# Attention scores as three products of 64 rows instead of two of 128, in pairs over the halves of the array, with turns and scores taken two by two

## The reference, cut to what matters

```python
q = x @ Wq + bq;  k = x @ Wk + bk;  v = x @ Wv + bv      # 8 heads of 64 columns
scores  = einsum('bdsh,bdth->bdst', q, k) / sqrt(8)       # 2048 x 2048 per head
weights = softmax(scores, axis=-1)
feats   = einsum('bdst,bdth->bdsh', weights, v)
x = layernorm(x + feats @ Wo + bo)
# then a mixture of experts: sigmoid gate, the best 6 of 64 experts, 256 places each,
# h = silu(g) * v of width 64, a shared expert of width 128, and a second layernorm
x = layernorm(x + shared + routed)
```

## Time and profile before

| what | value |
|---|---|
| runs, median (lowest to highest) | 1288.0 us (1287.32 to 1289.65) |
| the profiled execution, its own time | 1288.48 us |
| its span in the profile | 1286.7 us |
| busy share of the span | PE 97%, PEld 72%, DVE 69%, ACT 56%, POOL 30% |
| share of the chain that ended last | PE 88%, DVE 5%, DMA 3%, issue 2% |
| that chain by line | L1674 18%, L1642 17%, L1655 16%, L1476 11% and more |
| granted clock of TensorE | 0.996 of 2.4 GHz |

### The profile page before, as it was taken

One profiled execution on the slowest core, in us unless ns is written; L12 is line 12 of the kernel. 1 busy time (PEld: TensorE's weight loads), 2 busy tenths in 40 slices (PEclk: granted clock), 3 DMA queues, 4 the chain that ended last, 5 costly groups with the idle time before them and its releaser, 6 DMA issues.

```text
span 1286.7 us, 23210 instructions
## 1 busy us (share of the span) xinstructions
PE 1243.3 (97%) x8004; PEld 927.9 (72%) x8004; DVE 889.9 (69%) x1693; ACT 721.3 (56%) x1243; POOL 381.4 (30%) x434
## 2 busy tenths in 40 slices
PE   7999999999999999999999999999998999999896
PEld 5888777767777777767777777777766777777642
DVE  5622566667777868777767868767775777777387
ACT  5520366656555646646555655656623777787434
POOL 0000001212422322231331331331343666666412
PEclk9999999999999999999999999999998999999999
DMA  8788454534534543553543453563688999997598
GB/s 272 258 295 276 137 135 143 148 110 131 138 96 101 140 130 81 143 123 87 153 124 93 131 145 71 154 169 112 175 305 324 387 386 386 350 333 263 225 427 347
DMA packets 105059, 257.42 MB, mean 200 GB/s; under 512 B 26904, under 2 KB 53464, under 8 KB 101616
## 3 DMA queue, kind: packets, MB, share of 16 engines
q1 hardware_dynamic: 84720, 201.12, 50.3%
q0 software_dynamic: 17920, 50.62, 10.5%
q10 hardware_dynamic: 2304, 4.20, 0.8%
HBM read 182.26 MB, written 134.98 MB: 247 GB/s over the span
## 4 chain that ended last, share of the span: by engine, by line
PE 88%; DVE 5%; DMA 3%; issue 2%; POOL 1%; ACT 0%; SPq 0%; DVEq 0%; POOLq 0%; ACTq 0%
PE pv_acc L1674 18%; PE slot L1642 17%; PE slot L1655 16%; PE slot L1476 11%; PE slot L1740 5%; PE slot L1692 5%; PE misc L1538 4%; PE pv_acc L1476 3%; PE misc L1476 3%; PE slot L1782 2%; DMA got<-y_hbm 2%; DVE prob L1347 1%; DVE picked L1220 1%; PE misc L1583 1%; DVE base L1437 1%
## 5 line engine op out<-in xcount | busy, mean ns | idle before, releaser
L1004 ACT ACTIVATE prob<-prob,row_min 128x1024 f32<-128x1024 f32 x256 | 293.3, 1146 | 69.1 <-DVE prob L1347 62.5
L990 ACT ACTIVATE p_t<-slot 128x512 f32<-128x512 f32 x256 | 151.7, 592 | 293.1 <-PE slot L1642 291.4
L1655 PE MATMUL slot<-k_stack,q_stack 128*128 128x512 f32 x1024 | 299.9, 415 | 0.0
L1330 DVE COPY p_t<-slot 128x512 f32<-128x512 f32 x256 | 175.1, 684 | 165.7 <-PE slot L1642 164.5
L1642 PE MATMUL slot<-ident,prob 128*128 128x128 f32 x2048 | 269.3, 275 | 2.0 <-ACT prob L1004 2.0
L1642 PEld LDWEIGHTS slot<-ident,prob 128*128 128x128 f32 x2048 | 231.4, 141 | 52.4 <-issue 28.8
L1674 PE MATMUL pv_acc<-p_t,v_all 128*64 128x256 f32 x2048 | 235.2, 382 | 0.0
L1674 PEld LDWEIGHTS pv_acc<-p_t,v_all 128*64 128x64 f32 x2048 | 141.5, 137 | 90.8 <-issue 26.3
L844 POOL TENSOR_TENSOR moved<-acc,moved 64x256 f32<-64x256 f32 x63 | 46.0, 730 | 530.5 <-DMA moved<-acc 530.4
L1655 PEld LDWEIGHTS slot<-k_stack,q_stack 128*128 128x128 f32 x1024 | 173.7, 190 | 24.1 <-DVE p_t L1330 1.1
L1347 DVE TENSOR_SCALAR_CACHE_REDUCE prob<-slot,row_min 128x1024 f32<-128x1024 f32 x128 | 163.8, 1280 | 12.7 <-PE slot L1655 12.7
(11 more groups left out here) (196 smaller groups left out, 1698.8 us busy)
## 6 DMA issues: line engine op xcount, KB each, us to landing
disp_hbm<-zero_hbm SPq DMA_DIRECT2D x64, 518.0 KB, 6.2
rows_all<-disp_hbm SPq DMA_DIRECT2D x64, 518.0 KB, 9.6
y_hbm<-zero_hbm SPq DMA_DIRECT2D x48, 512.0 KB
got<-y_hbm SPq DMA_DIRECT2D x15, 1536.0 KB, 19.3
q_stack<-q_hbm SPq DMA_DIRECT2D x128, 128.0 KB, 4.5
up_pair<-in_L_ffn_w_up SPq DMA_DIRECT2D x26, 512.0 KB, 7.8
down_w<-in_L_ffn_w_down SPq DMA_DIRECT2D x32, 256.0 KB, 9.7
q_hbm<-q_hi SPq DMA_DIRECT2D x8, 512.0 KB, 2.8
```

The lines of the kernel that those rows point to most:

```text
L990: e.activation(p_t[m % 2][u][:, 0:2, :], view[:, 0:2, :], ACT.Copy).then_inc(a_pt, 1)
L1004: e.activation(keys, keys, ACT.Exp, bias=row_min[:, me % 2, j, 1:2], scale=-1.0, accum_out=row_sum[:, me % 2, j, half:half + 1]).then_inc( ...
L1330: e.tensor_copy(p_t[m % 2][u][:, 2:4, :], view[:, 2:4, :]).then_inc(v_pt, 1)
L1655: made = e.matmul(slot[:, n * BANK:(n + 1) * BANK], qs[:, part, j * P:(j + 1) * P], k_stack[:, ms % H, keys], start=part == 0, stop=part == 1)
```

## The change: what it does

- **Scores.** Each step has three products over 64 rows in place of two over 128: hi·hi, hi·lo and lo·hi (lo·lo is gone). The two banks of a step use different row halves of the array, and the matmuls alternate between them: 6 matmuls of 64 rows x 512 columns, each with its own weights.
- **Keys.** `k_rows` takes the place of `k_stack` with the same number of bytes. Keys for one bank lie in partitions 0 to 63 and for the other in 64 to 127. To get the shifted rows, the second half of each projection uses weights that are moved on by 64 columns; Wk is passed in with its first 64 columns repeated at its end (576 columns), and the bias with a rolled copy. ScalarE and VectorE write `k_rows` as 128 partitions x 512.
- **Order.** PE, DVE and ACT take two turns and then two scores, in even rounds only; the ring follows. Side jobs come between turns and scores, and after the scores. The two v pieces that are left for the attention come after the first two scores.
- **Around it.** Loads of the last chunk come up to 4 rounds later, since heads are done with their memory later; the load of pair 9 of the experts' weights also waits for the last projection, as that of pair 10 did.

```diff
@@ buffers
-        k_stack = sb("k_stack", [P, H, T], F32R, att)
+        k_rows = sb("k_rows", [P, H, 2, 2, BANK], F32R, att)
-        w_raw[0] = sb("w_raw0", [P, KC, C], F32, raw_k)
+        w_raw[0] = sb("w_raw0", [P, KC, C + D], F32, raw_k)
@@ order of the slots
-        for s in range(LAST + LAG):
-            takes += ([("turn", s - LAG)] if s >= LAG else []) + ([("scores", s)] if s < LAST else [])
-            takes += [("v", NS - V_LATE + s)] if s < V_LATE else []
+        for s in range(0, LAST + LAG, 2):
+            takes += [("turn", s - LAG), ("turn", s - LAG + 1)] if s >= LAG else []
+            takes += [("scores", s), ("scores", s + 1)] if s < LAST else []
+            takes += [("v", NS - V_LATE + s), ("v", NS - V_LATE + s + 1)] if s < V_LATE else []
@@ where keys lie
+        def keys_of(h, half, bank):
+            p, odd = divmod(h, 2)
+            place = 2 * p if bank == 0 else 2 * p + 1 if odd else 2 * ((p - 1) % (H // 2)) + 1
+            rows_at = slice(D, P) if odd != bank else slice(0, D)
+            return rows_at, [k_rows[rows_at, place, part, half, :] for part in range(2)]
         def keys_under_rows(n):
-            return (2 * (n + 1) * WITH - 1) // T
+            return min((2 * (n + 1) * WITH - 1) // T + 1, H - 1)
@@ SP, load_up and load_for_shared
-                if pair == 10:
+                if pair in (9, 10):
                     e.wait_ge(p_proj, 2 * NCH)
-                if s in (10, 14, 18):
+                if s in (14, 18, 22):
...
-                elif s == 23:
+                elif s == 27:
...
-                elif s == 24:
-                    head_used(e, 4)
+                elif s == 25:
+                    head_used(e, 5)
...
-                elif s == 26:
+                elif s == 29:
@@ ACT, keys (DVE's lo part likewise)
-                for odd in range(2):
-                    hi = slice(odd * D, (odd + 1) * D)
-                    e.activation(k_stack[hi, 2 * pair + odd, g * 2 * BANK:(g + 1) * 2 * BANK],
-                                 slot_of_take("k", n)[hi, :], ACT.Identity,
-                                 bias=bias_k[hi, pair:pair + 1]).then_inc(a_khi, 1)
+                for bank in range(2):
+                    e.activation(k_rows[:, 2 * pair + bank, 0, g, :],
+                                 slot_of_take("k", n)[:, bank * BANK:(bank + 1) * BANK], ACT.Identity,
+                                 bias=bias_k[:, bank, pair:pair + 1]).then_inc(a_khi, 1)
@@ DVE, copies of turned blocks (ACT likewise)
-                if 0 <= r < LAST:
-                    view = slot_of_take("turn", r)[:, :].rearrange("p (t q) -> p t q", t=4)
+                if 0 <= r < LAST and r % 2 == 0:
                     if m >= 2:
                         e.wait_ge(p_pv, m - 1)
-                    e.wait_ge(p_turned, 2 * r + 2)
-                    e.tensor_copy(p_t[m % 2][u][:, 2:4, :], view[:, 2:4, :]).then_inc(v_pt, 1)
+                    for i in range(2):
+                        view = slot_of_take("turn", r + i)[:, :].rearrange("p (t q) -> p t q", t=4)
+                        e.wait_ge(p_turned, 2 * (r + i) + 2)
+                        e.tensor_copy(p_t[m % 2][u + i][:, 2:4, :], view[:, 2:4, :]).then_inc(v_pt, 1)
@@ PE, projection of k
+                    first_col = pair * P + (half * D if name == "k" else 0)
+                    cols = slice(first_col, first_col + P)
@@ PE, attention
+            def score(s):
+                m, u = divmod(s, STEPS)
+                half, j = divmod(u, QT)
+                slot, qs = slot_of_take("scores", s), q_stack[m % 2]
+                e.wait_ge(d_q[m % 2], 32 * (m // 2 + 1))
+                for n in range(2):
+                    wait_bank(e, ("scores", s), n)
+                for i, (of_q, of_k) in enumerate(((0, 0), (0, 1), (1, 0))):
+                    for n in range(2):
+                        at, keys = keys_of(m % H, half, n)
+                        made = e.matmul(slot[:, n * BANK:(n + 1) * BANK], qs[at, of_q, j * P:(j + 1) * P], keys[of_k],
+                                        start=i == 0, stop=i == 2)
+                made.then_inc(p_scores, 1)
...
-                    for n in range(2):
-                        wait_bank(e, ("scores", s), n)
-                        keys = slice(half * HALF + n * BANK, half * HALF + (n + 1) * BANK)
-                        for part in range(2):
-                            made = e.matmul(slot[:, n * BANK:(n + 1) * BANK], qs[:, part, j * P:(j + 1) * P],
-                                            k_stack[:, ms % H, keys], start=part == 0, stop=part == 1)
-                    made.then_inc(p_scores, 1)
...
+                if 0 <= r < LAST and r % 2 == 0:
+                    turn(r)
+                    turn(r + 1)
+                side_step(jobs)
+                if s < LAST and s % 2 == 0:
+                    score(s)
+                    score(s + 1)
                     if s < V_LATE:
                         make_v(NS - V_LATE + s)
-                side_step(jobs)
+                        make_v(NS - V_LATE + s + 1)
@@ host
+        elif name == "L0_attn_bk":
+            a = np.stack([a.reshape(-1, P).T, np.roll(a, -P // 2).reshape(-1, P).T], 1)
...
+            if name == "L0_attn_Wk":
+                a = np.concatenate([a, a[..., :P // 2]], -1)
```

More of the change, by code:

```diff
@@ L123, in build @@
         w_hi, w_lo = [None] * 2, [None] * 2
-        w_hi[0], w_lo[0] = (sb(name, [P, KC, C], F32R, pro) for name in ("w_hi0", "w_lo0"))
+        w_hi[0], w_lo[0] = (sb(name, [P, KC, C + D], F32R, pro) for name in ("w_hi0", "w_lo0"))
         w_hi[1], w_lo[1] = (sb(name, [P, KC, C], F32R, pro) for name in ("w_hi1", "w_lo1"))
-        bias_k = sb("bias_k", [P, KC], F32, pro)
+        bias_k = sb("bias_k", [P, 2, KC], F32, pro)
         bias_q = sb("bias_q", [P, KC], F32, pro)
@@ L131, in build @@
         p_t = [[sb(f"p_t0{u}", [P, 4, QC], F32, att) for u in range(4)], p_over_x]
+        inv_all = [sb(f"inv_all{i}", [P, QC], F32, att) for i in range(2)]
         q_stack = [sb(f"q_stack{i}", [P, 2, QC], F32R, att) for i in range(2)]
@@ L165, in build @@
         feats.append(sb("feats1", [P, H // 2, QC], F32, att))
-        inv_all = [sb(f"inv_all{i}", [P, QC], F32, att) for i in range(2)]
         resid += [sb(f"resid{i}", [P, WITH], F32, att) for i in range(QT, 2 * QT)]
@@ L901, in split_weights @@
                     e.wait_ge(p_k, 8)
-                e.activation(w_hi[m % 2][:, ks, :], w_raw[m][:, ks, :], ACT.Copy).then_inc(a_whi, 1)
+                cols = slice(0, width_of(m))
+                e.activation(w_hi[m % 2][:, ks, cols], w_raw[m][:, ks, :], ACT.Copy).then_inc(a_whi, 1)
             def split_x(i):
@@ L1122, in vector @@
                 g, pair = divmod(n, H // 2)
[L1123 to L1126, removed]
+                for bank in range(2):
+                    e.wait_ge(a_khi, 2 * n + bank + 1)
                     e.scalar_tensor_tensor(
-                        out=k_stack[lo, h, tok], in0=slot_of_take("k", n)[hi, :], scalar=bias_k[hi, pair:pair + 1],
-                        in1=k_stack[hi, h, tok].bitcast(F32), op0=ALU.add, op1=ALU.subtract).then_inc(v_klo, 1)
+                        out=k_rows[:, 2 * pair + bank, 1, g, :],
+                        in0=slot_of_take("k", n)[:, bank * BANK:(bank + 1) * BANK],
+                        scalar=bias_k[:, bank, pair:pair + 1], in1=k_rows[:, 2 * pair + bank, 0, g, :].bitcast(F32),
+                        op0=ALU.add, op1=ALU.subtract).then_inc(v_klo, 1)
                 if n < 2:
@@ L1629, in chunk_end, with turn @@
                 yield from to(P1 + 30)
+            def turn(r):
+                m, u = divmod(r, STEPS)
+                view = slot_of_take("turn", r)[:, :].rearrange("p (t q) -> p t q", t=4)
+                wait_bank(e, ("turn", r), 0)
+                wait_bank(e, ("turn", r), 1)
+                e.wait_ge(a_exp, 4 * m + 2 * (u // 2) + 2)
+                for t in range(4):
+                    for j in range(QT):
+                        made = e.transpose(view[:, t, j * P:(j + 1) * P],
+                                           prob[:, m % 2, j, (4 * u + t) * P:(4 * u + t + 1) * P], ident[:, :])
+                    if t % 2:
+                        made.then_inc(p_turned, 1)
+            def score(s):
[11 more added lines that the diff above has]
+                made.then_inc(p_scores, 1)
             jobs = []
```

18 lines of the change are left out of this document (10 added, 8 removed).

## The result

| | before | after |
|---|---|---|
| median of the runs (lowest to highest), us | 1288.12 (1287.32 to 1289.65) | 1301.38 (1300.83 to 1305.68) |
| profiled execution, us (span) | 1288.5 (1286.7) | 1301.81 (1300.0) |
| first to last pv of the attention, us | 775.7 | 790.3 |
| PE busy / not busy in that stretch, us | 761.0 / 14.7 | 751.6 / 38.7 |

The ratio is 1.0114, with a 95% interval of 1.0094 to 1.0134. The forecast was 1280, in a range from 1262 to 1300; the median after the change lies just above that range. All of the loss is in the attention. The first pv starts at 158.73 us against 159.25 before, and what follows the last pv takes 351.0 us against 351.7.

A forecast was written before the change was run, and what follows sets the result against it. PE's own work was taken to bound the attention's 64 heads. At 0.13 us less each, 8.3 less, minus 0.3 for Wk's pieces, 8.0 came off 1288.5: 1280.5, as median 1280.0 us; range 1262 to 1300.

The forecast's parts named there:

- A pair on row halves costs 0.231: Scores on PE: two fp32r matmuls on row halves together cost one full matmul, 0.231 us, so 0.693 a step.
- serial pairs: Rival, scores on PE: the two matmuls of a pair take turns, 0.462 us a pair, 1440 us in total; chance 0.08.
- weights loaded before each pair: Rival, scores on PE: weight loads aren't hidden under the pair before, 12 x 0.10 us a head, 1339 us; chance 0.04.
- weight-load rule: PE's scores: a load overlaps a running matmul only when going to other rows, so each pair would also pay its load.
- Switches: PE between turns, scores and pv: 0.20 us into row halves, 0.15 out; new ones add 0.55 a head.
- PE alone: PE's own work in a plain head, without waits: 10.55 us against 10.95, 0.40 less.
- Start, prologue and tail: Outside the attention's heads: first turn starts as now, Wk's larger pieces cost 0.3 us, all behind the attention merely moves.
- Waits of 0.27 in a plain head: PE waits for VectorE before the third score, 0.18 us, and the fourth, 0.08; a plain head takes 10.82.
- Side jobs: Side work in each chunk of eight heads: between 0.3 us a head gained and 1.0 lost; taken as 0.
- gain of `picked`: PE's two waits of 1.1 us a chunk before the ranking, for VectorE's `picked`, go in the new order.
- the third rival: VectorE's ring delays a head's third and fourth score: 1325 us with all its side work there, 1295 with half; chance 0.16.
- 2.8 us a head in which VectorE idles: Argument against VectorE's ring being slower: it idles from the last read's end at 9.1 to the next copy.

The follow-up runs named there:

- side_grouped: `inverse_later` with side jobs stepped four at a time on PE, VectorE and ScalarE, only in rounds 2 and 3 of each head: 1256.32 us, ratio 0.9748.
- before_rank_later: The kernel before with one number changed, so PE takes the ranking one half round later: 1280.53 us, ratio 0.9949.
- inverse_later: The kernel after with VectorE's inverse of the row sums moved behind the second pair's copies, its store a round later: 1278.02 us, ratio 0.9918.
- bank_by_bank: The kernel after with a step's six score matmuls issued three for one bank, then three for the other: 1302.77 us in one profiled execution.
- order_alone: The kernel before with only the order changed to turn, turn, score, score; scores stay two products of 128 rows: 1311.99 us, ratio 1.0181.
- side_split: `side_grouped` with two of the four side steps that PE takes behind the pv moved before it: 1278.93 us, ratio 0.9937.

## Why the prediction was wrong, by its own steps

- **A pair on row halves costs 0.231: right.** Measured 0.230, with starts 1 to 7 ns apart in the first scores of a plain head. The rivals of serial pairs and of weights loaded before each pair didn't come. By this number the weight-load rule of the Trainium skill ("TensorE: Matmul & The Clock Gate", part 3) doesn't hold for these matmuls.
- **Switches: right.** Two turns took 1.90 = 2 x 0.87 + 0.15, two scores 1.60 = 6 x 0.23 + 0.20. PE alone at 10.55 a head fits `side_grouped`, whose plain head is 10.75 with about 0.1 of wait and 0.1 of weight load left, and the three heads of a chunk that gained 0.33 where 0.40 was PE's own saving.
- **Start, prologue and tail: right**, each within a microsecond. (The median before is 1288.12, so it lies 0.4 below the profiled execution, not 0.5.)
- **Waits of 0.27 in a plain head: right in place, a little small.** They were 0.36. The fourth score didn't only wait for the copy, it also had its first weight load uncovered: from its first pair to the second 0.31 passed instead of 0.23. A plain head gained 0.03, where 0.13 was forecast: 64 x 0.10 = 6.4 us.
- **The failed step is "Side jobs", where I took 0.** This step held that VectorE's side work would come out as waits before scores and that the gain of `picked` would pay for it. What the runs show in its place: the 8 plain heads came out as before, and the other 55 distances from pv to pv lost 14.8 us, 0.27 each. In the terms of the sum, this step is off by 16.5 us (14.8, and the 0.03 a head that these heads would have gained with the plain ones) and the waits of a plain head by 6.4, together the way from 8.3 less to 14.6 more in the attention. The cost is VectorE's place: PE stood idle for 24.0 us more, 38.7 for 14.7, while its busy time fell by only 9.4 of the 64 x 0.40 = 25.6. Of the missing 16.2 a part is waiting that the trace counts as busy, since a matmul of 0.39 reaches 0.16 into the wait behind it and the uncovered weight load follows (0.26 in a plain head), and about 3.4 is the two falls of the clock; the rest I didn't divide. The price of `picked` was misjudged too: in the old order, removing that wait gave 6.8 us (`before_rank_later`), not 14.
- **It is the third rival**, VectorE's ring, which had 0.16. At half of VectorE's side work it gave 1295, at all of it 1325; the time lies between. What I set against it, 2.8 us a head in which VectorE idles, was true and beside the point: it idles under the pv, while the copy in question comes at the end of its densest stretch. The argument was an average where a position was needed. The order in which VectorE's side jobs fall between read and copy could be read in the code, and the earlier trace rows together with the tick of the ranking would have priced much of it.
- **Not foreseen: long inverses.** The 18 at 0.60 to 0.86 sit in that same place, 14 of them in the first ranking head and the one behind it; the heads that hold the 18 gave 14.9 of the 23 us of `inverse_later`.
- **Not foreseen: two falls of the clock.** PE's granted clock went to half, 1.2 GHz, for 3.41 us at 436.90 and at 846.5, each time behind a wait like the one shown. The chain of waits around the first:

```profile
435.71 0.68 DVE p_t L1345
...
436.53 1.37 PE slot L1670 x6
...
438.11 4.70 PE pv_acc L1701 x32
```

The pv took 4.70 for 3.60. The head in which the clock fell and the one behind it are together 1.5 us longer than the same two heads of a chunk with as long an inverse (0.60 to 0.63) and no fall, so the two falls cost 3 us. The kernel before had none in the attention. That the waits brought them isn't shown: `bank_by_bank`, with the same waits (up to 1.2 us), had two as well, but `order_alone`, with waits of up to 0.96, had none.

That VectorE's order is the cause is shown by `inverse_later`, which changes it alone (with the store that follows the inverse) and leaves scores and turns as they are. `side_grouped` points the same way, but it also moves the side jobs of PE and ScalarE. Open is how the 45 us between `side_grouped` and the kernel after divide between VectorE's place and the work of PE that it let run under or behind the pv. The old order with grouped side jobs wasn't run either, so how much of the lead of `side_grouped` over the kernel before the new scores have isn't shown; 19 us is their share in the order of `side_split`.

## What to carry to other kernels

Where engines share a ring of few slots, write out for each slot which instruction frees it and everything that stands before that instruction on its engine, side jobs included; idle time elsewhere in the loop says nothing about it. Put small and occasional work behind the instruction that frees a slot, and its consumers behind the longest product: here moving a step of 0.27 us, 0.7 and more in 18 of 64 heads, gave 23 us, and grouping the rest 22 more. Count a switch of the array's tiling as an operation (0.20 in, 0.15 out) and batch the work so that few are left.

## What the runs showed of the hardware

- Two row halves run beside each other even when their matmuls aren't issued alternately (`bank_by_bank`: pairs every 0.230 us, one execution). By that pace PE started a matmul of the other half ahead of ones queued before it.
- The first pair behind a wait on a semaphore took 0.31 to the next instead of 0.23. I read the 0.08 as its weight load, no longer covered; no run isolated it.
- A VectorE tensor_tensor of 128 x 2 took 0.16 in most cases and 0.60 to 0.86 in 18 of 64 in the kernel after, each time beside a GpSimd tensor_tensor. GpSimd's side of the case at 296.04 (the second timeline of VectorE above):

```profile
295.97 0.72 POOL L856 TENSOR_TENSOR moved<-acc,moved 64x256 f32<-64x256 f32 x1 [9.92 <-DMA moved<-acc]
```

Six such inverses stayed short beside the same line, and no run took the neighbour away: seen, not shown as a cause.
